# First layer: where VectorE's collapse of an output stands among the low parts of the probabilities

## What is computed

```
a = _layer_norm(audio_kv, ln_gamma, ln_beta)
Q = hidden_states @ Wq.T ; K = a @ Wk.T ; V = a @ Wv.T      # split into 16 heads of 16
scores = einsum('bhtd,bhsd->bhts', Q, K) * scale
attn = softmax(scores, axis=-1)
out = einsum('bhts,bhsd->bhtd', attn, V)
return hidden_states + tanh(gate) * (out @ Wo.T)
```

## Time and profile before

| | us |
|---|---|
| median of 3 runs | 1791.48 |
| lowest, highest | 1789.04, 1791.99 |
| profiled execution | 1799.13 |
| its span, first to last instruction | 1797.3 |
| busy in it: PE, PEld | 1672.9, 1576.3 |
| busy in it: DVE, ACT, POOL | 1203.6, 1041.9, 902.7 |
| first and last collapse begin at | 80.9, 459.8 |

### The profile page before, as it was taken

One profiled execution on the slowest core, in us unless ns is written; L12 is line 12 of the kernel. 1 busy time (PEld: TensorE's weight loads), 2 busy tenths in 40 slices (PEclk: granted clock), 3 DMA queues, 4 the chain that ended last, 5 costly groups with the idle time before them and its releaser, 6 DMA issues.

```text
span 1797.3 us, 36860 instructions
## 1 busy us (share of the span) xinstructions
PE 1672.9 (93%) x12520; PEld 1576.3 (88%) x12520; DVE 1203.6 (67%) x2340; ACT 1041.9 (58%) x2023; POOL 902.7 (50%) x655
## 2 busy tenths in 40 slices
PE   4788988997899999999999999999999999999997
PEld 3677877786789999999999987889999999999986
DVE  5577777777356766766766766466676677677673
ACT  2467766676264655656656555545665656556563
POOL 4456665542144545536535547453653554455483
PEclk8899999999699999999999999899999999999998
DMA  7967666746221111111211114221121121120031
GB/s 211 234 161 183 180 173 177 179 115 167 73 81 62 54 50 37 64 41 36 70 35 36 70 32 131 62 85 37 36 70 36 35 70 36 36 70 1 2 91 40
DMA packets 109995, 150.81 MB, mean 84 GB/s; under 512 B 25540, under 2 KB 95684, under 8 KB 109828
## 3 DMA queue, kind: packets, MB, share of 16 engines
q1 hardware_dynamic: 108484, 142.45, 28.4%
q10 hardware_dynamic: 1344, 6.19, 1.0%
HBM read 108.32 MB, written 3.42 MB: 62 GB/s over the span
## 4 chain that ended last, share of the span: by engine, by line
PE 67%; DVE 10%; ACT 3%; issue 2%; SPq 1%; POOL 1%; DMA 1%; ACTq 0%; DVEq 0%; POOLq 0%
PE ps L770 12%; PE ps L772 11%; PE ps L771 11%; PE ps L1025 7%; PE ps L1029 7%; PE ps L1027 7%; PE ps L960 2%; DVE ar L1866 2%; PE ps L1005 2%; PE ps L992 1%; DVE neg L1742 1%; PE ps L853 1%; PE ps L870 1%; DVE ar L1911 1%; ACT prob L1299 1%
## 5 line engine op out<-in xcount | busy, mean ns | idle before, releaser
L722 POOL TENSOR_TENSOR rr<-ar,rr 125x512 fp32r<-125x512 f32 x336 | 455.3, 1387 | 406.6 <-ACT rr L1483 398.7
L1025 PE MATMUL ps<-cx,rr 125*128 125x258 f32 x1344 | 396.6, 295 | 0.0
L1029 PE MATMUL ps<-cx,rr 125*128 125x258 f32 x1344 | 379.6, 282 | 0.0
L1027 PE MATMUL ps<-cx,rr 125*128 125x256 f32 x1344 | 379.3, 282 | 0.0
L770 PE MATMUL ps<-rr,ct 128*125 128x256 f32 x1152 | 329.6, 286 | 4.5 <-DVE ar L1911 2.7
L772 PE MATMUL ps<-rr,ct 128*125 128x256 f32 x1152 | 324.7, 282 | 0.0
L771 PE MATMUL ps<-rr,ct 128*125 128x256 f32 x1152 | 324.7, 282 | 0.0
L1470 ACT ACTIVATE ar<-ar 125x512 f32<-125x512 f32 x336 | 208.5, 626 | 84.5 <-DVE ar L1911 59.4
L1027 PEld LDWEIGHTS ps<-cx,rr 125*128 125x128 f32 x1344 | 254.9, 190 | 0.0
L1029 PEld LDWEIGHTS ps<-cx,rr 125*128 125x128 f32 x1344 | 254.8, 190 | 0.0
L1025 PEld LDWEIGHTS ps<-cx,rr 125*128 125x128 f32 x1344 | 253.6, 189 | 0.1
(11 more groups left out here) (210 smaller groups left out, 3778.6 us busy)
## 6 DMA issues: line engine op xcount, KB each, us to landing
raw_t<-in_ctx_t SPq DMA_DIRECT2D x24, 1500.0 KB, 6.7
k<-khl SPq DMA_DIRECT2D x192, 187.5 KB
raw<-in_ctx SPq DMA_DIRECT2D x16, 1500.0 KB
raw<-in_ctx SPq DMA_DIRECT2D x8, 1408.0 KB
raw<-stat_scratch ACTq DMA_DIRECT2D x7, 750.0 KB, 3.9
w_raw<-in_wq SPq DMA_DIRECT2D x32, 128.0 KB, 2.3
w_raw<-in_wk SPq DMA_DIRECT2D x32, 128.0 KB, 2.2
qo<-in_wqt SPq DMA_DIRECT2D x32, 128.0 KB, 3.2
```

Source lines behind the costliest of these rows:

```text
L722: pool.tensor_tensor(group(p[:, 1, :, :], u, k), x, f(group(p[:, 0, :, :], u, k)), ALU.subtract)\
L1025: pe.matmul(ps[:, bank, 0:D + 2], hi, cx[0:KC, c, 0:D + 2], start=c == 0, stop=False, skip_group_check=True)
L1027: pe.matmul(ps[:, bank, 0:D], hi, cx[0:KC, c, D + 2:CW], start=False, stop=False, skip_group_check=True)
L1029: mm = pe.matmul(ps[:, bank, 0:D + 2], lo, cx[0:KC, c, 0:D + 2], start=False, stop=c == CH - 1, skip_group_check=True)
```

## The change

In VectorE's `slot`, the call of `collapse` for the pair before moves behind the low parts 0 and 1 of the present pair. Nothing is added or removed. The two calls behind the last slot (`low_probs(GT0 - 1, 2)`, `collapse(B - 1, SLOTS - 1, GT0 - 1)`) stay as they are.

```
                 if kind == "plain" and t == SLOTS - 1:
                     reciprocals(b, n)
+                low_probs(g, 0)
+                low_probs(g, 1)
                 if t or later:
                     collapse(b if t else b - 1, (t - 1) % SLOTS, g - 1)
-                low_probs(g, 0)
-                low_probs(g, 1)
                 if kind == "full" and t == 0:
                     load_stats(b + 2, 0)
```

## The result

The changed kernel takes 1810.21 us, the median of 4 runs (1808.42 to 1814.93), against 1790.74 us (4 runs, 1789.04 to 1791.99) for the kernel before: a ratio of 1.0106, interval 1.0086 to 1.0126, so 19 us slower. Two later comparisons, each with both kernels on one chip, gave 1.0084 (1.0056 to 1.0111, 15.1 us) and 1.0102 (1.0077 to 1.0127, 19.9 us). One execution of the kernel before in a later comparison took 3216.52 us, in a slow state, and is left out. The forecast was 1800.6, 9.1 slower, with a range to 1804.5: the direction was right, the size was not.

A forecast was written before the change was run, and what follows sets the result against it. TensorE was busiest but waited for the third low part, whose time VectorE's row maximum set in some slots. Delays of 2.6 + 1.4 + 2.5 + 2.6 = 9.1 us on 1791.48 gave 1800.6 us, range 1795.7 to 1804.5.

The forecast's parts named there:

- the late row maxima: VectorE-bound slots 1, 5 and 6 and the plain batch: row maxima delayed by the moved collapse, 9.1 us in all.
- Step 1: VectorE's low parts, with the collapse out of the way, start 0.09 us earlier; 0.20 in the loop kept for the range.
- Step 2: Row maximum behind the moved collapse: costs 0.46 us (even) or 0.58 (odd), less 0.09: 0.37 or 0.49 later.
- step 3: Slot-by-slot costs: nothing in slots 7, 0, 2, 3 and keys-batch slots 1 to 4; elsewhere 9.1 us in sum.
- Slack called enough: Keys batch, slots 1 to 4: row maxima 0.2 to 0.3 us later, but TensorE a block of keys ahead; cost nothing.
- Step 4: TensorE's `weighted` waits for the collapse, now ending about 206.0 instead of 204.54; hidden, with 0.8 us of cover left.
- The rival of the clock: Longer TensorE idle times bring more half-clock stretches, 1.6 us each; two more give 1803.8 us. Chance 0.13.
- Faster: Low parts come earlier and TensorE, idling ahead of its third transposes or `weighted`, uses it: 1787.2 us. Chance 0.05.
- absorbed: A late row maximum is made up in the next slot; only the plain batch pays 2.6 us: 1794.1. Chance 0.12.
- Carrying the 7.65 us: Profiled execution lay 7.65 us above the median; that difference was carried over, turning 1808.2 into 1800.6 us.

The follow-up runs named there:

- filled kernel with the halves turned: Changed kernel with each collapse's two instructions in the other order and 8 unneeded products in TensorE's waits for the third low part: 1795.15 us, ratio 1.0018.
- filled changed kernel: Changed kernel with 8 unneeded products added on TensorE in its waits for the third low part: 1800.96 us, ratio 1.0061.
- The turned halves: Changed kernel with the two instructions of each collapse in the other order, lower partitions last: 1803.78 us, ratio 1.0070.

## Why the prediction was right or wrong

The measured 19.5 us in these terms: the late row maxima cost 7.5 (0.4 of it in the batch with keys, priced at nothing), where the forecast said 9.1; the hold that it did not price in these places costs 4.3 to 5.0 more; some 7 are left, for which the clock is the likely reason. With all slots at what they measured the forecast would have been 1804.1 (1791.48 + 12.6), still inside its range; it is the rest that carries the time out of it.

- **Where the time is bound, and where the wait goes.** Right. The collapse's wait was cover for the high parts; with the collapse gone the same idle time stands ahead of the low parts (78.0 us).
- **Step 1, the gain of the low parts.** Right in kind, and in size where nothing else came in between. In the filled kernel with the halves turned, the last batch's slots are 0.37 to 0.48 longer, as forecast (0.37 and 0.49). In the loop the gain was nearer to the 0.20 that the forecast kept for its range than to the 0.09 that it took: slot 1's row maximum is 0.37 later, 0.58 - 0.20, and slots 5 and 6 together 0.33 to 0.39, where 0.20 + 0.37 was forecast and 0.58 - 0.20 - 0.29 = 0.09 plus 0.46 - 0.20 = 0.26 would have been right. Outside the loop it is 0.49 at slot 1, as forecast, and 0.50 to 0.52 for slots 5 and 6 together. This is most of what makes 7.5 out of the 9.1.
- **The gain taken away again.** In the changed kernel itself the last batch's slots are 0.46 and 0.58 longer, step 2 without step 1. TensorE, then ScalarE, then VectorE of the filled changed kernel:

```profile
438.67 0.60 PE L870 MATMUL ps<-pt,v 128*66 128x224 f32 x4 [0.66 <-DVE pt L1672]
439.11 0.93 PE L853 MATMUL ps<-ident,prob 112*128 112x112 f32 x8
```

```profile
439.46 0.24 ACT L1310 ACTIVATE ost<-ps 64x112 f32<-64x112 f32 x1
439.69 0.98 ACT L1252 ACTIVATE pt<-ps 128x448 fp32r<-128x448 f32 x2
```

```profile
436.15 1.72 DVE L1747 TENSOR_REDUCE neg<-ps 112x1 f32<-112x1500 f32 x1
437.90 0.62 DVE L1672 TENSOR_TENSOR pt<-ps,pt 128x448 fp32r<-128x448 f32 x1
440.27 1.16 DVE L1672 TENSOR_TENSOR pt<-ps,pt 128x448 fp32r<-128x448 f32 x2 [1.75 <-ACT pt L1252]
```

The row maximum at 436.15 has its third low part at 437.90, 1.75 later. TensorE's last products of `weighted` follow at 438.67, its transposes at 439.11, and ScalarE's high part 0 starts at 439.69, 0.23 after `ost` where it was 0.15 after it in the kernel before (423.35 in the earlier trace rows):

```profile
423.20 0.24 ACT L1305 ACTIVATE ost<-ps 64x112 f32<-64x112 f32 x1
```

The transposes, themselves later by the late low part, most likely hold it up. The low part then starts 0.58 after its high part, where 0.57 was forecast, but from a later high part: nearly the whole gain of 0.09 is gone.
- **Step 2, the order cost of the row maximum.** Right: 0.46 and 0.58.
- **The step that failed: "Nothing"** in step 3 for slots 7, 0 and 3 and for the batch with keys; slot 4, which cost the same, is not in its list at all. (Slot 2 did cost nothing.) The collapse now stands ahead of the row maximum, and the row maximum reads PSUM only. The last read of SBUF before the third low part is thus the collapse's read of `ost` from partitions 32 to 63, and the low part, which reads from partition 0 on, is held until the row maximum has ended. In the old order the two low parts stood between and no start was lost. That is 0.12 us in front of the very instruction that TensorE waits for, in 56 of 62 slots: 4.3 to 5.0 us in all. The rule in the Trainium skill's page VectorE: DVE Perf Modes, section Two Vector instructions with no wait between them, says just this, that the last start is kept for each memory by the last instruction that read it. The forecast cited the rule and used it for the neighbours of the collapse alone. The turned halves agree with the rule, both for the low part and for the row maximum behind even pairs. The forecast also held the starts 0.09 ahead of an end against the section The DRAIN you can't avoid; the section goes on to say that an instruction that is not held starts earlier, so they are no evidence against it.
- **Slack called enough.** Two slots of the batch with keys (pairs 2 and 4) cost 0.2 each, where TensorE's room was judged by one slot and not by what the next one left of it.
- **Step 4, the added wait.** Right: hidden but for 0.3 us at most.
- **The rival of the clock** was the second failure: the sum has no term for it. It was given as an alternative, with 0.13 and 3.2 us, while it adds to the sum: the changed kernel's runs lack 4 to 11 us of clock more. With TensorE's waits filled the lack is the same in both kernels to 1.3 us and the difference is 12.4. That the clock is what the other comparisons have on top is likely and not shown: the unfilled changed kernel was never timed beside the filled ones, the lowest of the three comparisons (15.1) cannot be told from 12.4, and the traces do not show which stretches account for it. It stays open.
- **Faster and absorbed** fell: no slot of the changed kernel that saw no clock change got shorter by more than 0.05 us. The sign that "faster" named was there, TensorE's transposes waiting for low parts, and these waits did shrink, from 4.2 us in 11 to 1.1 us in 5 (100 to 350 us), but the time was not set there.
- **Carrying the 7.65 us** from the first trace to the median did no harm to the difference, but two of the changed kernel's three traces lay below their medians, and the first trace of before above its own. A difference of two single traces (9.9 us there) is no estimate of the times.

## What to carry to other kernels

Before moving a small instruction that seems to waste a wait, ask what released the work behind it: a wait that already covers another one yields next to nothing, and the instruction then costs its whole length where nothing covers it. And look two instructions on, not one: on VectorE what the moved instruction read, from which partitions, can delay the start of the next one that reads the same memory, which may be the one that TensorE waits for. Where two orders of the same instructions are free, end with the one whose partitions the next reader shares; here that was worth 4.3 to 5.0 us of slots in the changed kernel and nothing measurable in the kernel before.

## What the runs showed of the hardware that was not expected

- A third low part started 0.12 us earlier or later (1.63 or 1.75 us after the row maximum) by nothing but which half of the collapse came last, with another instruction of 1.72 us in between.
- The collapse's cost is mostly fixed: two instructions of 32 by 56 took 0.42 us, of 32 by 1 still 0.30.
- 1 us of products that nobody needs, put into 27 places where TensorE idled 1.2 to 1.9 us, kept its clock at the upper level from 100 to 455 us in all four traces with them, where it fell at least once in each of the ten without. With 29 more at the layer's end and the halves turned the kernel was 0.34% faster.
